# Linear attention and a routed FFN on one core: the bias added between scatter and return, and z of two batches computed ahead

## The chip, the core and the metric

The kernel runs on one core of a Trainium2 chip. The metric is the device time of one execution in microseconds. The engines are named as the profile names them: PE (TensorE, with PEld for its weight loads), DVE (VectorE), ACT (ScalarE), POOL (GpSimd) and SP (SyncE, which here only issues DMAs).

## What is computed

x is 4096 tokens of 128 numbers. Everything is float32.

```python
xn = layernorm(x)
# attention: 16 heads of 8 dims, 32 features a head; B = 16, T = 256
q, k, v = split(xn @ w_qkv)
q_prime = exp(z_q - max(z_q)), k_prime = exp(z_k - max(z_k))   # z = einsum('bhtd,hdf->bhtf', ., proj)
kv = einsum('bhtf,bhtd->bhfd', k_prime, v);  k_sum = sum(k_prime, axis=t)
att = (q_prime @ kv) / (q_prime @ k_sum + 1e-6);  A = att @ w_out + b_out
# FFN: 8 experts, 256 wide, Sinkhorn routing (3 iterations), top 2 of 8
gates = sinkhorn((xn @ router_w.T + router_b) / temp);  two best, weights sum to 1
F = xn + sum over the two of weight * ((relu(xn @ wg[e]) * (xn @ wp[e])) @ wo[e])
return x + A + F
```

## The kernel before

The 4096 tokens are 32 tiles of 128 (NT); a batch is two tiles, and there are 16 (NB). `acc` holds x of all tiles in SBUF and collects the result. Each engine runs its own list of instructions in program order and waits on semaphores; nothing is scheduled by a tool, so the order written in the code is the order that runs.

*Head (0 to 24 us).* x is loaded and normalised, xn is transposed and split in a high and a low part (three products make one product of nearly float32 precision), and the weights of the features are folded: `w_feat_high`, `w_feat_low`.

*Routing (24 to 60 us).* The Sinkhorn iterations and the top-2 choice are one chain of small instructions that goes round PE, DVE and ACT (`route_link`, links 0 to 17). It is interleaved with attention's steps for b = -1 and b = 0. At its end DVE places every token: `slot_i` gives each of the 2 x 4096 rows a slot in `slots_x` in HBM, sorted by expert, in 39 tiles of 256 slots (SLOT_TILES, ST).

*Attention (60 to 169 us).* `step(b, ...)` on each engine works on batch b and, ahead of it, on batch f = b + 1. In the names of the trace: `z(n, f)` is one of four groups of three 128x512 matmuls on PE (L618 to L620; n = 0, 1 for k, n = 2, 3 for q) into PSUM bank Z_BANK + n; DVE takes its negated maximum (`z_max`, L1058) and adds it (`z_shift`, L1065) into `z_sb`; ACT's exponential (`features`, L871) gives `feat`. For batch b, `kv(b)` is 16 matmuls of 36 columns (L642), `qT` transposes feat 2 and 3 (L656), ACT copies them out (`copy_qT`, L882), `numden(b)` is 16 matmuls of 36 columns (L666), DVE divides (`att`, L1080 to L1090) in the next step, PE transposes att (L673), ACT copies (L888), PE multiplies with w_out (`project`, L682) and DVE adds the product to `acc` (L1101, counted in `acc_added`). `kv(b)` waits for att of b - 1, since both use bank 6. 14 batches run so (EARLY); batches 14 and 15 run behind the experts.

Beside this, POOL scatters the rows: 64 indirect DMAs of 128 rows (L532), each followed by `add_xn`, half a tile of acc += xn (L491). Each waits on z_shifted, so that they keep pace with attention.

*Experts (169 to 272 us).* SP loads the weights of each tile's expert (`load_weights` into one of six `w_tile`, 384 KB) and its rows (`load_rows`, `x_tile`). PE transposes the rows and makes the up and gate products (L783 to L785) and the down product (L795); ACT splits (L948, L952), applies relu (L962) and scales the result into `y_tile` (L969, counted in `y_scaled`); DVE splits (L1262, L1281 `w_low`) and multiplies (L1270). POOL returns the rows: `send_rows(k)`, two indirect DMAs of 128 rows (L541) into `rows_y` in token order. Among them POOL adds the bias: 64 half tiles (`add_bias`, L496), one or two behind nearly every DMA, and a memset of one column of `gap` (L546) behind each tile. PE, ACT and DVE don't wait for a tile's return until 16 tiles later (YR).

*End (272 to 325 us).* PE runs attention's batches 14 and 15. SP waits for all returns (`y_sent`), reads both planes of rows back, POOL and DVE add them to acc (L327), and SP and ACT store it.

`keep_warm` (L574) is matmuls on constants whose result nobody reads.

## Time and profile before

| | us |
|---|---|
| median of 3 runs | 329.74 (328.19 to 330.65) |
| the profiled execution | 327.3 |
| its span in the trace | 325.5 |

| engine | busy us | share of the span | instructions |
|---|---|---|---|
| PE | 274.7 | 84% | 2044 |
| PEld | 257.5 | 79% | 2044 |
| DVE | 222.9 | 68% | 523 |
| ACT | 160.3 | 49% | 365 |
| POOL | 237.6 | 73% | 388 |

Of the chain of work that ended last, the page gives PE 49%, POOL 23%, DVE 12%, DMA 6%, ACT 2%. Times of a row are microseconds from the start of the span. An instruction's busy time on PE overlaps that of its neighbours, so the pace of PE is read from start to start. "PEclk" is the clock granted to PE as a share of 2.4 GHz.

### The profile page before, as it was taken

The numbers are of one execution on the slowest core, as the hardware profiler recorded it, in microseconds if no ns is written. First come the engines' busy times: TensorE is split into PE (matmuls) and PEld (weight loads), VectorE is DVE, ScalarE is ACT, GpSimd is POOL, SyncE is SP. The second block draws the span as 40 slices with busy tenths as digits, with TensorE's granted clock in tenths as the row PEclk, the third lists the DMA queues.
The fourth block names the chain that finished last, engine by engine and source line by source line (L and its number), as shares of the span: only waits on it lengthen the run. The fifth ranks groups of instructions, "written<-read, shape, count | busy, mean of one in ns | idle before, by whom it ended". The sixth has DMA issues, their size and how long they took to land.

```text
span 325.5 us, 6627 instructions
## 1 busy us (share of the span) xinstructions
PE 274.7 (84%) x2044; PEld 257.5 (79%) x2044; DVE 222.9 (68%) x523; ACT 160.3 (49%) x365; POOL 237.6 (73%) x388
## 2 busy tenths in 40 slices
PE   5996878799999999999699999999999999850020
PEld 4896777689999999999599999999999999850010
DVE  4948889668888778888855777777777774500173
ACT  2774562134555555455346677777777775210000
POOL 5899520757888888888611688888888888888381
PEclk9998996589999999999979999999999999885555
DMA  7974000551111111111142598898888841111694
GB/s 236 339 272 164 4 0 0 167 191 45 47 50 52 45 49 46 47 50 51 36 110 61 166 244 245 244 256 251 245 246 248 251 134 48 42 49 40 226 383 174
DMA packets 32462, 45.22 MB, mean 139 GB/s; under 512 B 5328, under 2 KB 21200, under 8 KB 32432
## 3 DMA queue, kind: packets, MB, share of 16 engines
q1 hardware_dynamic: 26592, 33.83, 34.1%
q0 software_dynamic: 4544, 9.84, 9.0%
q10 hardware_dynamic: 1296, 1.20, 1.1%
q8 instruction: 13, 0.21, 0.3%
q14 instruction: 17, 0.14, 0.1%
HBM read 27.17 MB, written 17.68 MB: 138 GB/s over the span
## 4 chain that ended last, share of the span: by engine, by line
PE 49%; POOL 23%; DVE 12%; DMA 6%; issue 5%; ACT 2%; SPq 1%; ACTq 0%; POOLq 0%; DVEq 0%
POOL rows_y L541 17%; PE bank L642 7%; PE bank L666 6%; POOL acc L496 5%; PE bank L618 4%; PE bank L619 4%; PE bank L620 4%; PE bank L656 4%; PE bank L795 3%; DMA xn<-rows_y 2%; PE bank L591 2%; PE bank L783 2%; PE bank L574 2%; PE bank L784 2%; PE bank L785 2%
## 5 line engine op out<-in xcount | busy, mean ns | idle before, releaser
L541 POOL DMA_INDIRECT rows_y<-xn,row_i x78 | 80.5, 1032 | 28.2 <-ACT xn L969 15.1
L532 POOL DMA_INDIRECT slots_x<-xn,slot_i x64 | 63.9, 999 | 29.4 <-DVE slot_i L1195 10.1
L871 ACT ACTIVATE feat<-z_sb 128x512 f32<-128x512 f32 x64 | 39.9, 631 | 65.7 <-DVE z_sb L1065 65.7
L1058 DVE TENSOR_REDUCE neg_max<-bank 128x16 f32<-128x512 f32 x64 | 42.7, 684 | 19.8 <-PE bank L620 19.8
L783 PE MATMUL bank<-xT_high,w_high 128*128 128x256 f32 x156 | 47.3, 303 | 0.5 <-issue 0.5
L785 PE MATMUL bank<-xT_high,w_low 128*128 128x256 f32 x156 | 44.0, 282 | 0.0
L784 PE MATMUL bank<-xT_low,w_high 128*128 128x256 f32 x156 | 44.0, 282 | 0.0
L1065 DVE TENSOR_TENSOR z_sb<-bank,neg_max 128x512 f32<-128x512 f32 x64 | 42.6, 684 | 0.5
L795 PE MATMUL bank<-w_tile,hidden 128*128 128x128 f32 x312 | 41.0, 275 | 0.0
L642 PEld LDWEIGHTS bank<-v_aug,feat 128*128 128x128 f32 x256 | 31.5, 200 | 8.8 <-issue 7.4
L795 PEld LDWEIGHTS bank<-w_tile,hidden 128*128 128x128 f32 x312 | 38.2, 192 | 0.1
L969 ACT ACTIVATE xn<-bank,x_tile 128x128 f32<-128x128 f32 x78 | 24.5, 365 | 25.8 <-PE bank L795 25.8
L642 PE MATMUL bank<-v_aug,feat 128*128 128x36 f32 x256 | 31.9, 283 | 5.7 <-DVE att L1090 5.7
L1281 DVE TENSOR_TENSOR w_low<-w_tile,w_high 128x512 fp32r<-128x512 f32 x39 | 28.5, 734 | 4.5 <-ACT w_high L952 1.2
L666 PE MATMUL bank<-kv_sb,qT_sb 128*128 128x36 f32 x256 | 31.6, 282 | 0.0
L666 PEld LDWEIGHTS bank<-kv_sb,qT_sb 128*128 128x128 f32 x256 | 31.5, 201 | 0.0
L1262 DVE TENSOR_TENSOR xT_low<-bank,xT_high 128x256 fp32r<-128x256 f32 x39 | 16.5, 424 | 21.8 <-ACT xT_high L948 21.8
L618 PE MATMUL bank<-w_feat_high,xnT_high 128*128 128x512 f32 x64 | 31.2, 487 | 0.0
L783 PEld LDWEIGHTS bank<-xT_high,w_high 128*128 128x128 f32 x156 | 29.6, 190 | 0.7 <-issue 0.7
L784 PEld LDWEIGHTS bank<-xT_low,w_high 128*128 128x128 f32 x156 | 29.8, 191 | 0.0
L785 PEld LDWEIGHTS bank<-xT_high,w_low 128*128 128x128 f32 x156 | 29.6, 190 | 0.0
L1270 DVE TENSOR_TENSOR hidden<-bank,gate_act 128x512 f32<-128x512 f32 x39 | 26.5, 680 | 3.2 <-PE bank L785 3.2
(145 smaller groups left out, 562.5 us busy)
## 6 DMA issues: line engine op xcount, KB each, us to landing
w_tile<-w_expert_dram SPq DMA_DIRECT2D x39, 384.0 KB
slots_x<-w_tile SPq DMA_DIRECT2D x39, 144.0 KB, 2.2
x_tile<-slots_x SPq DMA_DIRECT2D x39, 130.0 KB
acc<-x_dram SPq DMA_DIRECT2D x8, 256.0 KB, 5.3
xn<-rows_y SPq DMA_DIRECT2D x8, 256.0 KB, 5.8
w_tile<-rows_y SPq DMA_DIRECT2D x8, 256.0 KB, 6.5
rows_y<-xn,row_i POOLq DMA_INDIRECT x78, 3.7
slots_x<-xn,slot_i POOLq DMA_INDIRECT x64, 2.3
```

Source lines behind the costliest of these rows:

```text
L532: pool.indirect_dma_start(slots_x, bass.IndirectOffsetOnAxis(slot_i[k][:, i:i + 1], 0), xn[:, j, :], None).then_inc(scattered[n % FLIGHT], 16)
L541: pool.indirect_dma_start(rows_y, bass.IndirectOffsetOnAxis(row_i[:, k, t:t + 1], 0), y_tile(k, t), None)\
L618: pe.matmul(to, xT(xnT_high, f, half), w_feat_high[:, qk, :], start=True, stop=False)
L642: mm = pe.matmul(bank[KV_BANK][:, c * AUG:(c + 1) * AUG], feat[par][h][:, c * P:(c + 1) * P], v_aug[:, 2 * b + h, c * AUG:(c + 1) * AUG], ...
L666: mm = pe.matmul(bank[KV_BANK][:, at:at + AUG], qT_sb[h][:, c * P:(c + 1) * P], kv_sb[par][:, c, :], start=True, stop=True)
L783: pe.matmul(to, w_high[n][:, cols], xT_high[n][:, :], start=True, stop=False)
L784: pe.matmul(to, w_high[n][:, cols], xT_low[n][:, :], start=False, stop=False)
L785: mm = pe.matmul(to, w_low[n][:, cols], xT_high[n][:, :], start=False, stop=True)
L795: mm = pe.matmul(y_bank(r, t), hidden[r % UP][:, c, t * P:(t + 1) * P], w_tile[:, r, at:at + D], start=(c == 0), stop=(c == FC - 1))
L871: act.activation(feat[par][n][:, :], z_sb[n][:, :], ACT.Exp).then_inc(feat_ready, 1)
L1058: dve.tensor_reduce(neg_max[n][:, :], args(n), AX_X, ALU.max, negate=True).then_inc(z_negmax, 1)
L1065: dve.tensor_tensor(z_sb[n][:, :].rearrange("p (h f) -> p h f", f=F), args(n), wide(neg_max[n], F), ALU.add).then_inc(z_shifted, 1)
```

## The change

It has two parts.

The bias. `add_bias` becomes a group of four tiles (128x512), eight of them, which POOL runs behind the last `add_xn` and ahead of the first `send_rows`; the groups wait for acc_added 2, 4, ... 12, 13, 13. Between the return DMAs no bias add is left, and behind each of the 78 DMAs stands a memset of one column.

z of batches 4 and 9 (AHEAD). `z_ahead(i)`, i = 0 to 7, makes the eight groups of three matmuls in idle banks (QT_BANK, V_BANK) during routing: 0 to 2 ahead of the row transposes of the three iterations, 3 and 4 behind the transposes of batch 0, 5 to 7 behind numden(0). ACT copies each to SBUF (`store_ahead`): batch 4 into w_tile, batch 9 into hidden and gate_act. In the attention stage `z(n, 4)` and `z(n, 9)` are left out on PE, and DVE reads the stored ones. SP's first weight load now waits for z_shifted 20 (batch 4's z used up), since it overwrites the store.

```diff
+    AHEAD = (4, 9)
-        gap = sb("gap", [P, SLOT_TILES])
+        gap = sb("gap", [P, 2 * SLOT_TILES])
+        z_store = [flat_w[:, FEAT * (n + 1):FEAT * (n + 2)] for n in range(4)]
+        z_store += [t[:, :, :].rearrange("p c s -> p (c s)") for t in hidden] + [gate_act[1][:, :]]
...
+            sp.wait_ge(z_shifted, 4 * (AHEAD[0] + 1))
             for k in range(LOOP):
                 load_weights(*ahead(k, 0, 0))
...
-            def add_bias(n):
-
-                j, cols = half_tile((n + 4 * (EARLY - 1)) % (2 * NT))
-                pool.tensor_tensor(acc[:, j, cols], acc[:, j, cols], b_out_sb[:, cols], ALU.add).then_inc(bias_added, 1)
+            def add_bias(g):
+
+                tiles = acc[:, g * GROUP:(g + 1) * GROUP, :]
+                pool.tensor_tensor(tiles, tiles, over_tiles(b_out_sb, GROUP), ALU.add).then_inc(bias_added, 1)
...
-                    n = 2 * k + t
-                    for piece in range(n * NT // SLOT_TILES, (n + 1) * NT // SLOT_TILES):
-                        add_bias(piece)
-                pool.memset(gap[:, k:k + 1], 0.0)
+                    pool.memset(gap[:, 2 * k + t:2 * k + t + 1], 0.0)
 
             pool.wait_ge(base_added, 2 * NT)
+            for g in range(NG):
+                pool.wait_ge(acc_added, min(GROUP // 2 * (g + 1), EARLY - 1))
+                add_bias(g)
             pool.wait_ge(acc_added, EARLY - 1)
...
             def z(n, f):
 
+                if f in AHEAD:
+                    return
...
+            def z_ahead(i):
+
+                n, f = i % 4, AHEAD[i // 4]
+                pe.wait_ge(xnT_split, f // 2 + 1)
...
+                z_products(n, f, z_ahead_bank(i)[:, :]).then_inc(z_ahead_ready, 1)
...
                     values(2 * (n // 5))
+                    z_ahead(n // 5)
                     pe.wait_ge(row_normed, n // 5 + 1)
...
                 if back:
                     qT(0, b, par, route)
+                if back and route:
+                    z_ahead(3)
...
                 if back:
                     qT(1, b, par, route)
+                if back and route:
+                    z_ahead(4)
...
                 if back:
                     numden(b, par)
+                if back and route:
+                    for i in range(5, 8):
+                        z_ahead(i)
...
+            def store_ahead(i):
+
+                act.wait_ge(z_ahead_ready, i + 1)
+                act.copy(z_store[i], z_ahead_bank(i)[:, :]).then_inc(z_ahead_stored, 1)
...
-            def args(n):
-                return bank[Z_BANK + n][:, :].rearrange("p (h f) -> p h f", f=F)
+            def args(n, f):
+                z = z_store[4 * AHEAD.index(f) + n] if f in AHEAD else bank[Z_BANK + n][:, :]
+                return z.rearrange("p (h f) -> p h f", f=F)
```

Of PE's list, the second half of step 3 (batch 3, ahead of it f = 4), before: the last of att's transposes, then the transposes of feat 2 and 3 with z(2) and z(3) between them, the projection, and numden of batch 3.

```order
L673 MATMUL bank0<-ident,att 128x128 x2
L656 MATMUL bank5<-ident,feat1_2 128x128 x4
L618 MATMUL bank3<-w_feat_high,xnT_high 128x512
L619 MATMUL bank3<-w_feat_low,xnT_high 128x512
L620 MATMUL bank3<-w_feat_high,xnT_low 128x512
L656 MATMUL bank7<-ident,feat1_3 128x128 x4
L618 MATMUL bank4<-w_feat_high,xnT_high 128x512
L619 MATMUL bank4<-w_feat_low,xnT_high 128x512
L620 MATMUL bank4<-w_feat_high,xnT_low 128x512
L682 MATMUL bank5<-w_out_sb,attT 128x128 x2
L666 MATMUL bank6<-kv_sb1,qT_sb0 128x36 x4
```

Both z groups are gone from here, and so are z(0) and z(1), which stood between numden of batch 2 and kv of batch 3; the same holds for step 8. In the changed kernel PE goes from numden(2) straight to kv(3).

Of PE's list in step 0, behind kv(0), now: the transposes of feat 3 (L695), then z_ahead(4), the two products of the routing counts (L735, L736), numden(0) (L705), and the first of z_ahead(5) to (7), ahead of z(0) and z(1) of batch 2.

```order
L695 MATMUL bank<-ident,feat_3 128x128 x4
L653 MATMUL bank<-w_feat_high,xnT_high 128x512
L654 MATMUL bank<-w_feat_low,xnT_high 128x512
L655 MATMUL bank<-w_feat_high,xnT_low 128x512
L735 MATMUL bank<-mask,earlier_r 128x256
L736 MATMUL bank<-mask,ones_r 128x256
L705 MATMUL bank<-kv_sb,qT_sb 128x36 x8
L653 MATMUL bank<-w_feat_high,xnT_high 128x512
L654 MATMUL bank<-w_feat_low,xnT_high 128x512
L655 MATMUL bank<-w_feat_high,xnT_low 128x512
```

Before, the counts followed the transposes at once, and behind numden(0) stood only the six matmuls of z(0) and z(1); now there are fifteen.

Of POOL's list in the middle of the expert stage, before: return DMAs (L541), bias adds of half a tile (L496), and the memset behind a tile (L546).

```order
L541 DMA rows_y<-xn,row_i 18176x128
L496 TENSOR_TENSOR acc<-acc,b_out_sb 128x64
L546 MEMSET gap 128x1
L541 DMA rows_y<-xn,row_i 18176x128 x2
L496 TENSOR_TENSOR acc<-acc,b_out_sb 128x64
```

And the same list now, with its start:

```order
L506 TENSOR_TENSOR acc<-acc,xn 128x64
L511 TENSOR_TENSOR acc<-acc,b_out_sb 128x512 [waits acc_added,base_added]
L511 TENSOR_TENSOR acc<-acc,b_out_sb 128x512 [waits acc_added] x7
L556 DMA rows_y<-xn,row_i 18176x128 [waits y_scaled,rows_numbered,acc_added]
L558 MEMSET gap 128x1
L556 DMA rows_y<-xn,row_i 18176x128
L558 MEMSET gap 128x1
L556 DMA rows_y<-xn,row_i 18176x128 [waits y_scaled,rows_numbered]
```

The 64 small adds have become eight large ones ahead of the first return, and the memsets are 78 instead of 39.

## Rows read from the trace of the kernel before

**Rows 1.** Busy time by stages: stretch, its length, engines, PEclk, DMA share, GB/s

```profile
60.20:169.10 108.90, 106.17 (x748) 97.13 (x748) 85.60 (x169) 51.05 (x94) 83.82 (x130) 0.95 0.22 70
169.10:272.00 102.90, 102.28 (x881) 101.80 (x880) 72.53 (x156) 73.29 (x191) 80.99 (x135) 1.00 0.73 210
272.00:302.20 30.20, 16.40 (x118) 15.24 (x117) 7.40 (x15) 5.89 (x12) 25.46 (x47) 0.80 0.14 44
```

**Rows 2.** POOL's timeline (start, duration, line, tiles, idle before): tiles 0, 1, 38

```profile
177.61 0.98 POOL L541 DMA_INDIRECT rows_y<-xn,row_i  x1 [12.74 <-ACT xn L969]
...
182.41 0.98 POOL L541 DMA_INDIRECT rows_y<-xn,row_i  x1 [2.10 <-ACT xn L969]
...
298.44 0.99 POOL L541 DMA_INDIRECT rows_y<-xn,row_i  x1 [0.16 <-issue]
```

**Rows 3.** ACT's timeline: y of two tiles in a row, and of tile 38

```profile
250.16 0.63 ACT L969 ACTIVATE xn<-bank,x_tile 128x128 f32<-128x128 f32 x2 [0.64 <-PE bank L795]
...
252.71 0.63 ACT L969 ACTIVATE xn<-bank,x_tile 128x128 f32<-128x128 f32 x2 [0.64 <-PE bank L795]
...
272.24 0.63 ACT L969 ACTIVATE xn<-bank,x_tile 128x128 f32<-128x128 f32 x2 [0.42 <-PE bank L795]
```

**Rows 4.** POOL's timeline: two return DMAs with only the memset between

```profile
276.32 0.99 POOL L541 DMA_INDIRECT rows_y<-xn,row_i  x1 [0.17 <-issue]
277.32 0.11 POOL L546 MEMSET gap<- 128x1 f32 x1
277.62 0.96 POOL L541 DMA_INDIRECT rows_y<-xn,row_i  x1 [0.19 <-issue]
```

**Rows 5.** Timeline of all engines: a return DMA behind DVE's w_low

```profile
213.40 0.69 DVE L1281 TENSOR_TENSOR w_low<-w_tile,w_high 128x512 fp32r<-128x512 f32 x1
213.57 1.39 POOL L541 DMA_INDIRECT rows_y<-xn,row_i  x1 [0.16 <-issue]
```

**Rows 6.** DVE's timeline: the first add of returned rows

```profile
307.66 0.89 DVE L327 TENSOR_TENSOR acc<-xn,acc 128x512 f32<-128x512 f32 x1 [19.86 <-DMA xn<-rows_y]
```

**Rows 7.** Groups of POOL by form: count | busy, mean ns | idle before

```profile
L327 POOL TENSOR_TENSOR acc<-xn,acc 128x512 f32<-128x512 f32 x4 | 5.7, 1414 | 5.5 <-DMA xn<-rows_y 5.4
```

**Rows 8.** PE's timeline in a steady step: numden, z(0), kv, next numden

```profile
107.91 1.87 PE L666 MATMUL bank<-kv_sb,qT_sb 128*128 128x36 f32 x16
109.61 0.48 PE L618 MATMUL bank<-w_feat_high,xnT_high 128*128 128x512 f32 x1
...
111.09 1.87 PE L642 MATMUL bank<-v_aug,feat 128*128 128x36 f32 x16
...
115.75 0.42 PE L666 MATMUL bank<-kv_sb,qT_sb 128*128 128x36 f32 x3
```

**Rows 9.** Who waited for whom: total us, times, longest

```profile
PE bank L701 <- DVE row_log L1143: 4.8, 3, 2.5
```

**Rows 10.** PE in two stretches: length, PE busy, PEclk, DMA share, GB/s

```profile
51.00:68.00 17.00, 14.56 (x56) 0.50 0.41 140
283.00:286.50 3.50, 3.50 (x18) 0.51 0.12 37
```

**Rows 11.** PE's timeline: kv(1) and numden(1)

```profile
60.21 3.60 PE L642 MATMUL bank<-v_aug,feat 128*128 128x36 f32 x16 [1.80 <-DVE att L1090]
...
68.66 1.87 PE L666 MATMUL bank<-kv_sb,qT_sb 128*128 128x36 f32 x16
```

**Rows 12.** Timelines of DVE and ACT in the steady step: att, the second qT copy

```profile
110.43 0.42 DVE L1090 TENSOR_TENSOR att<-bank,inv_den 128x256 f32<-128x256 f32 x1
...
114.81 0.59 ACT L882 COPY qT_sb<-bank 128x512 f32<-128x512 f32 x1
```

**Rows 13.** PE's timeline: numden(14), kv(15), numden(15)

```profile
278.10 1.87 PE L666 MATMUL bank<-kv_sb,qT_sb 128*128 128x36 f32 x16
...
281.19 1.95 PE L642 MATMUL bank<-v_aug,feat 128*128 128x36 f32 x16 [1.22 <-DVE att L1090]
...
287.85 1.87 PE L666 MATMUL bank<-kv_sb,qT_sb 128*128 128x36 f32 x16
```

More of the change, by code:

```diff
@@ L251, in by_token_tile, with z_ahead_bank, in_psum @@
             return t.rearrange("p (j d) -> p j d", d=P)
+        flat_w = w_tile[:, :, :].rearrange("p r n -> p (r n)")
+        z_store = [flat_w[:, FEAT * (n + 1):FEAT * (n + 2)] for n in range(4)]
+        z_store += [t[:, :, :].rearrange("p c s -> p (c s)") for t in hidden] + [gate_act[1][:, :]]
+        def z_ahead_bank(i):
+            return bank[QT_BANK if i < 3 or i % 2 == 1 and i > 4 else V_BANK]
+        def in_psum(f):
+            return f - sum(1 for a in AHEAD if a < f)
         def v_bank(g):
@@ L934, in step @@
                     copy_qT(0, b, route)
+                if back and route:
+                    store_ahead(3)
                 if tail:
@@ L938, in step @@
                     copy_qT(1, b, route)
+                if back and route:
+                    for i in range(4, 8):
+                        store_ahead(i)
                 if front and not route:
@@ L1097, in add_projection @@
                 dve.wait_ge(base_added, 4 * b + 4)
[L1098 to L1099 removed]
+                if b == EARLY - 1:
+                    dve.wait_ge(bias_added, NG)
                 tiles = acc[:, bass.ds(2 * b, 2), :]
```

40 lines of the change are left out of this document (29 added, 11 removed).

## The prediction

> **What bounds the kernel now.** I read the table by stages first. The attention stage (60.2 to 169.1 us) has PE busy 106.17 of 108.90 us, the expert stage PE 102.28 of 102.90 us, and behind it stand 30.2 us with PE busy 16.40 us and POOL 25.46 us [rows 1], then, up to 325.5, 23.3 us of reading back, adding and storing. So two things decide: when the experts can start (PE in the attention stage), and when POOL has sent the last of the 39 tiles' rows back. POOL's timeline shows that it is POOL, not PE, that ends the expert stage: tile 0 is sent at 177.61 after 12.74 us of idling, tile 1 at 182.41, tile 38 at 298.44, while ACT had tile 38 ready at about 272.87 [rows 2, 3]. Between tiles 1 and 38 lie 37 tiles in 116.03 us, 3.136 us each; PE makes one in 2.55 us (252.71 less 250.16). POOL falls some 25 us behind.
>
> **Term A, the returns.** A tile is two indirect DMAs. 64 of the 78 DMAs have a bias add behind them; where only the memset stands there, the way from DMA to DMA, 276.32 to 277.62, is 1.30 us [rows 4]. The change leaves only that form: 2.60 us a tile. On top come collisions: the DMA at 213.57 started inside DVE's w_low (213.40, 0.69 us, both inputs in SBUF) and took 1.39 instead of 0.99 us [rows 5]. At 2.60 us against DVE's 2.55 the two drift by 0.05 us a tile, so that one of the two DMAs of a tile runs into w_low about every 6 to 12 tiles and pays 0.4 to 0.6 us: 0.06 us a tile. I take 2.66: 37 x (3.136 - 2.66) = **-17.6 us**. Bounds: no collisions, 2.60, -19.8 us; one hit of 0.40 in every tile, 3.00, -5 us. PE doesn't cap it (2.55 is less), nor does what comes after: DVE's first add of returned rows, at 307.66, comes after 19.86 us of idling [rows 6]. The Trainium skill (SBUF — State Buffer, "SBUF: two separate sides") has the pair of ports that DVE and GpSimd share as a lock held for the whole instruction against a DVE instruction with two SBUF inputs; the row of 1.39 us agrees, and by that rule too the sum stays near 2.66 a tile.
>
> The eight bias adds now stand between the last scatter's add and tile 0. POOL's nearest form, 128x512 with two inputs, takes 1.41 us [rows 7]: 11.3 us, six of which may start at once, two when acc_added reaches 13. They fall into the 12.74 us that POOL idles [rows 2]. Cost nothing; if they run 2 us over, tile 1 still comes 4.8 us after tile 0 and takes it up.
>
> **Term B, the routing.** Eight z products are added (24 matmuls, a group of three is 0.70 us, from half of the 1.48 us between 109.61 and 111.09, [rows 8]) and eight ACT copies of 0.57 us. Three groups stand ahead of the row transposes, where PE waits 4.8 us in three waits [rows 9]: hidden, and the copies fit into ACT's gaps. The other five stand between the transposes of batch 0 and the z of batch 2, while DVE is placing the slots. There PE now runs at 1.2 GHz: the granted clock is 0.50 from 51 to 68 us [rows 10], so that kv(1) at 60.21 needs until numden at 68.66 to arrive, 8.45 us where the same way takes 4.66 (111.09 to 115.75) [rows 8, 11]. If the added matmuls hold the clock, up to 3.8 us come back; if it falls anyway, nine more matmuls at 0.43 us end about 62, 1.8 us after kv(1) wants to start. I take **-1.5 us**. The weight loads now wait for z_shifted 20, some 30 us later; they are wanted at 157.
>
> **Term C, batches 4 and 9 without z on PE.** The intent is 12 matmuls less, 2.9 us, in a PE-bound step of 7.85 us (107.91 to 115.75) [rows 8]. But look at who waits in the step. z(0) and z(1) run from 109.61 to 111.09 [rows 8]; kv behind them also waits for att, which DVE ends at 110.85 [rows 12]. Taking the six away brings kv 0.15 us forward. The same with z(2), z(3): numden waits for ACT's second qT copy, which stands in ACT's order behind two exponentials and two copies; it ended at 115.40 [rows 12], against numden at 115.75, and could go 0.25 us earlier. So the step sheds 0.5 us, not 2.9. DVE's own work doesn't get less: it reads z from SBUF instead of PSUM, same shapes.
>
> What it does to the clock is worse. Without z a step is numden, a gap, kv, a few transposes, a gap, numden. The trace has one such step, batch 15: numden(14) at 278.10, 1.22 us idle, kv at 281.19, numden(15) at 287.85: **9.75 us, longer than a step with z (7.85)**, though six filling matmuls stand in for the twelve of z [rows 13]. The granted clock is 0.51 from 283.0 to 286.5, right behind numden, gap and kv [rows 10]. The other low stretch, 51 to 68, was not ended by the z of batch 2, between a numden and a kv at half clock, and ended in the dense run of transposes and z of batch 2 ahead of numden(1). In the middle of the attention stage a fallen clock hits a PE-bound stretch: numden +1.7, the next z(0), z(1) +1.4, kv +1.7, the rest up to z(3) about +2 until the clock is back. That is 3 to 8 us a time; less the 0.5 us shed, I take +5 a batch, **+10 us** for both. Bounds per batch: -0.5 (no fall) and +8.
>
> The Trainium skill (TensorE: Matmul & The Clock Gate, "HAM oscillation") ties the fall to PE standing idle between bursts of matmuls. In a step without z PE would still be busy most of the time, and by that rule alone the clock holds; batch 15's rows say otherwise. What the rule gives is the first rival.
>
> **Sum.** 327.3 (the profiled execution; span 325.5) - 17.6 - 1.5 + 10 = 318.2 us. That execution lies 2.4 us under the median of the three timed ones (329.74), so for a median I say **320 us**.
>
> **Rivals.**
> *The clock holds in both batches*: C is -1, and B nearer -2.5: 327.3 - 17.6 - 2.5 - 1 = 306.2, 308.5 for a median. For it: a steady step keeps 1.00 with numden and kv in it. Against: batch 15.
> *The clock falls and stays down over whole steps* (slower than before): every us at half clock costs 0.5 us of a PE-bound stage, so 38 us of low clock eat the 19 us won. In the trace the longest low stretch is 17 us; two of 30 us, from numden and kv of a following batch keeping it down, would give 327.3 - 19.1 + 30 = 338.
> *The returns don't get faster*: as POOL sends faster the DMA engines, busy 0.73 in the expert stage [rows 1], deliver x_tile rows late and PE paces at 3 us, or collisions hit every tile: A is -5 or less: 327.3 - 5 - 1.5 + 10 = 330.8, 332 for a median.
>
> **Chances.** My forecast (returns faster, clock falls at 4 and 9) 0.60, clock holds 0.23, stays down 0.08, returns no faster 0.09. About 1% is what a measurement of this kernel can tell from no change. The forecast's own range is 312 (both falls short) to 327 (both long, A at -15). The overall range must reach the first rival: 307 to 328. Faster by over 1% (below 326.4): 0.56 + 0.23 = 0.79; within 1%: 0.04 + 0.08 = 0.12; slower: 0.08 + 0.01 = 0.09.
>
> **What would show it.** A: return DMAs 1.30 us apart, POOL done about 7 us behind ACT's last y rather than 26. B: the clock of 51 to 68 and the distance from kv(1) to numden(1). C: the distance from numden(2) to numden(3) and to numden(4), and the granted clock there: 7.4 and 7.85 at full clock mean the first rival, 9 and 12 or more mean my step. The end of the attention stage (PE's filling matmuls, 169.1) should come about 8 us later; if it comes earlier than 168, term C is wrong. If the DMAs stay 1.5 us apart, term A is.

## The result, and the profile after

The changed kernel takes **348.31 us** (median of 4 executions, 340.10 to 353.88) where the kernel before, run beside it, takes 328.97 (327.89 to 330.65): ratio **1.041, 95% interval 1.026 to 1.056**. Ratios, here and below, leave out executions more than 1.5% above the fastest of their kernel (here 353.88, the profiled one, and 351.71; the other two, 340.10 and 344.92, give 1.041), while medians have all of them. It is slower; 320 us and "faster" were predicted. The experiments showed more than that sign. They ran on five chips (which chip the two kernels of this section ran on is not known). On one of them the same changed kernel is 4% *faster* than the kernel before, and on another its bias part alone is 6% faster. What differs between the chips is the subject of most of what follows.

The profiled execution of after has 353.88 us (span 352.1, mean granted clock 0.890), that of before had 327.3 (0.909). The first view to read is, in both, the line that scales an expert tile's result on ACT: its group says when the first and the last of the 78 halves started. Before:

```profile
L969 ACT ACTIVATE xn<-bank,x_tile x78: 358/365/370, 176.2 to 272.5; 128x128 f32<-128x128 f32 x78
```

The same line of after, and who it waited for (total us, times):

```profile
L1029 ACT ACTIVATE xn<-bank,x_tile x78: 358/368/407, 191.6 to 318.5; 128x128 f32<-128x128 f32 x78
its engine sat idle before it (us, times) until:
  PE bank L844: 18.1, 14
  remote: 17.2, 10
```

The extra 26.6 us of this execution fall into three pieces. The first scaled tile comes 15.4 us later (191.6 against 176.2), which is the attention stage. From the first to the last scaling it takes 126.9 us in place of 96.3, 30.6 more. And from there to the end it takes 33.6 us in place of 53.0, 19.4 less, since POOL is no longer far behind. 15.4 + 30.6 - 19.4 = 26.6.

The attention stage on PE, where [rows 11] and [rows 8] answer (start, duration, group of matmuls, idle before; L677 is kv, L705 numden, L589 the filling matmuls at the stage's end):

```profile
59.03 2.94 PE L677 MATMUL bank<-v_aug,feat 128*128 128x36 f32 x16 [2.51 <-DVE att L1154]
...
66.99 1.87 PE L705 MATMUL bank<-kv_sb,qT_sb 128*128 128x36 f32 x16
...
74.83 1.87 PE L705 MATMUL bank<-kv_sb,qT_sb 128*128 128x36 f32 x16
...
77.93 1.95 PE L677 MATMUL bank<-v_aug,feat 128*128 128x36 f32 x16 [1.22 <-DVE att L1154]
...
82.77 3.47 PE L705 MATMUL bank<-kv_sb,qT_sb 128*128 128x36 f32 x16
...
97.46 1.87 PE L705 MATMUL bank<-kv_sb,qT_sb 128*128 128x36 f32 x16
```

And PE in four stretches of after (length, busy us of PE, PEld, DVE, ACT, POOL, granted clock as a share of 2.4 GHz, DMA share, GB/s), where [rows 1] and [rows 10] answer:

```profile
59.80:66.60 6.80, 6.80 (x28) 6.11 (x28) 3.17 (x6) 3.20 (x6) 4.33 (x8) 0.50 0.14 47
80.20:97.30 17.10, 16.95 (x69) 15.28 (x68) 8.82 (x18) 6.39 (x13) 10.04 (x16) 0.50 0.51 174
124.60:145.10 20.50, 20.41 (x85) 18.74 (x85) 10.64 (x20) 7.16 (x13) 12.15 (x18) 0.50 0.10 34
184.70:318.50 133.80, 110.35 (x880) 105.70 (x880) 70.44 (x156) 73.86 (x192) 82.84 (x149) 0.97 0.56 166
```

Behind batch 2 and behind batch 7 the clock falls to 1.2 GHz and stays there for 17.1 and 20.5 us, with PE busy throughout. In the last row PE is busy 110.35 of 133.80 us: in the expert stage, where it was never idle before, it now waits for 23 us, with the clock at 0.97 and with the DMA engines less busy than before (0.56; 0.77 from 176.0 to 272.5 before).

POOL does what the change is for. Its timeline, where [rows 2] and [rows 4] answer, and two of the waits:

```profile
178.71 9.90 POOL L511 TENSOR_TENSOR acc<-acc,b_out_sb 128x512 f32<-128x512 f32 x8
193.02 0.98 POOL L556 DMA_INDIRECT rows_y<-xn,row_i  x1 [4.41 <-ACT xn L1029]
194.00 0.12 POOL L558 MEMSET gap<- 128x1 f32 x1
194.31 0.96 POOL L556 DMA_INDIRECT rows_y<-xn,row_i  x1 [0.19 <-issue]
```

```profile
POOL rows_y L556 <- ACT xn L1029: 38.8, 28, 4.4
```

The eight adds take 9.90 us inside POOL's idle time, the return DMAs stand 1.29 us apart, and POOL now waits for scaled tiles (38.8 us in 28 waits) where it had been 25 us behind them.

### The profile page after: what moved, and what is told of

It reads as the page before. It is cut to its first block, busy times and chain, and to the rows that moved or that the text cites. A ratio compares the mean times of both kernels' runs of the same rounds, so it can differ in the third digit from the quotient of the medians.

```text
span 352.1 us, 6625 instructions
## 1 busy us (share of the span) xinstructions
PE 298.9 (85%) x2044; PEld 275.5 (78%) x2044; DVE 220.8 (63%) x523; ACT 165.6 (47%) x373; POOL 227.8 (65%) x371
## 4 chain that ended last, share of the span: by engine, by line
PE 56%; DVE 15%; ACT 10%; issue 9%; another core or an unknown queue 6%; DMA 3%; ACTq 0%; DVEq 0%
PE bank L677 9%; PE bank L705 6%; PE bank L844 5%; PE bank L695 4%; PE bank L653 4%; PE bank L655 4%; PE bank L654 3%; PE bank L832 3%; PE bank L834 3%; PE bank L833 3%; PE bank L589 2%; ACT xn L1029 2%; ACT w_high L1012 2%; PE bank L723 2%
## 5 line engine op out<-in xcount | busy, mean ns | idle before, releaser
L556 POOL DMA_INDIRECT rows_y<-xn,row_i x78 | 75.7, 971 | 51.9 <-ACT xn L1029 38.8
L1122 DVE TENSOR_REDUCE neg_max<-bank 128x16 f32<-128x512 f32 x56 | 37.6, 685 | 27.3 <-PE bank L655 27.2
L832 PEld LDWEIGHTS bank<-xT_high,w_high 128*128 128x128 f32 x156 | 30.3, 194 | 26.2 <-DVE xT_low L1326 19.5
L677 PEld LDWEIGHTS bank<-v_aug,feat 128*128 128x128 f32 x256 | 38.0, 233 | 11.6 <-issue 9.8
L677 PE MATMUL bank<-v_aug,feat 128*128 128x36 f32 x256 | 38.2, 314 | 9.0 <-DVE att L1154 9.0
L1129 DVE TENSOR_TENSOR z_sb<-bank,neg_max 128x512 f32<-128x512 f32 x56 | 37.2, 682 | 0.4
L705 PE MATMUL bank<-kv_sb,qT_sb 128*128 128x36 f32 x256 | 33.3, 290 | 1.9 <-ACT qT_sb L936 1.9
L705 PEld LDWEIGHTS bank<-kv_sb,qT_sb 128*128 128x128 f32 x256 | 33.2, 210 | 2.1 <-ACT qT_sb L936 2.1
L653 PE MATMUL bank<-w_feat_high,xnT_high 128*128 128x512 f32 x64 | 32.6, 510 | 0.1
L1022 ACT ACTIVATE gate_act<-bank 128x512 f32<-128x512 f32 x39 | 23.7, 607 | 17.9 <-PE bank L834 11.2
L936 ACT COPY qT_sb<-bank 128x512 f32<-128x512 f32 x32 | 18.6, 582 | 27.0 <-PE bank L695 24.0
L834 PEld LDWEIGHTS bank<-xT_high,w_low 128*128 128x128 f32 x156 | 30.6, 196 | 0.0
```

What stands on the lines that cost most here:

```text
L556: pool.indirect_dma_start(rows_y, bass.IndirectOffsetOnAxis(row_i[:, k, t:t + 1], 0), y_tile(k, t), None)\
L653: pe.matmul(to, xT(xnT_high, f, half), w_feat_high[:, qk, :], start=True, stop=False)
L677: mm = pe.matmul(bank[KV_BANK][:, c * AUG:(c + 1) * AUG], feat[par][h][:, c * P:(c + 1) * P], v_aug[:, 2 * b + h, c * AUG:(c + 1) * AUG], ...
L705: mm = pe.matmul(bank[KV_BANK][:, at:at + AUG], qT_sb[h][:, c * P:(c + 1) * P], kv_sb[par][:, c, :], start=True, stop=True)
L832: pe.matmul(to, w_high[n][:, cols], xT_high[n][:, :], start=True, stop=False)
L834: mm = pe.matmul(to, w_low[n][:, cols], xT_high[n][:, :], start=False, stop=True)
```

## The experiments

The trace also holds a record of each semaphore increment. I read `y_ready`, which the last matmul of a tile's `down` raises, and call a tile's signal late when the increment comes more than 0.45 us behind that matmul's end. (In before it comes 0.29 us behind the matmul's start, which is its end, in all 39 tiles; where the expectations give 0.29 us as behind the end, they are loose.) ScalarE's scaling and SyncE's next weight load both wait for it. After has 19 late signals of 39, by 38 us in sum. Where records of `y_ready` are missing (1 in after, up to 5 in before_third, ahead_only, ahead_only_again and bias_dummy_adds), an increment is matched to the nearest matmul, so a count or a sum there can be off by a few. "Remote" as a releaser stands in such rows where the profile could join the increment to no matmul, since it came too long behind its end: bias_only has it 13 times in front of the scaling, and all its records of `y_ready`.

### One part at a time

bias_only: the kernel before with the bias part alone.

```diff
+            for g in range(NG):
+                pool.wait_ge(acc_added, min(GROUP // 2 * (g + 1), EARLY - 1))
+                add_bias(g)
...
-                    for piece in range(n * NT // SLOT_TILES, (n + 1) * NT // SLOT_TILES):
-                        add_bias(piece)
-                pool.memset(gap[:, k:k + 1], 0.0)
+                    pool.memset(gap[:, 2 * k + t:2 * k + t + 1], 0.0)
```

> The kernel before with the change's bias part alone: the eight bias adds between scatter and return, a one-column memset behind each of the 78 return DMAs, and no z ahead of its turn. In the trace of the changed kernel the expert stage on TensorE takes 133 us in place of 103, and TensorE's signals there (y_ready by line 844) reach ScalarE 2 to 3 us after the matmuls end in 19 of 39 tiles, where the kernel before has 0.29 us in all 39. Theory R (the returns that now follow each scaled tile in step disturb this stage): this kernel shows the same late signals, an expert stage of 120 to 133 us, and a time of 325 to 345 us although the returns start earlier. Theory Z (z ahead of its turn, or the clock that falls behind it, is the cause of all of it): an expert stage of 103 us, returns 2.66 us a tile, and about 312 us, the 17.6 us of the prediction's first term off the 329.

Measured: **340.71 us** against 331.12 (ratio 1.027, 1.016 to 1.037), 18 late signals, scalings from 178.5 to 307.5. Theory R: the steps of the attention stage take 7.84 us as before, and the part that I had counted on for -17.6 us costs 10.

ahead_only: the changed kernel with the bias adds back among the returns.

```diff
-            for g in range(NG):
-                pool.wait_ge(acc_added, min(GROUP // 2 * (g + 1), EARLY - 1))
-                add_bias(g)
...
-                    pool.memset(gap[:, 2 * k + t:2 * k + t + 1], 0.0)
+                    n = 2 * k + t
+                    for piece in range(n * NT // SLOT_TILES, (n + 1) * NT // SLOT_TILES):
+                        add_bias(piece)
+                pool.memset(gap[:, k:k + 1], 0.0)
```

> The changed kernel with its bias part undone: the bias adds stand among the returns as before, one memset for a pair of return DMAs, but z of batches 4 and 9 is still computed during routing. Theory R: no late signals in the expert stage, which takes 103 us again; what is left is the slower attention stage (+15.4 us in the trace of the changed kernel) less 1.7 us of routing, so about 340 to 345 us. Theory Z: the expert stage stays at 120 to 133 us and the time is 350 us or more.

Measured: 336.50 us (ratio 1.013, 1.000 to 1.026), and 22 late signals, scalings from 181.1 to 302.7. So neither theory as I had put it: without the bias part the signals are late as well, and the time is still under 340.

bias_only_one_gap: as bias_only, with one memset for a pair of return DMAs.

```diff
-                    pool.memset(gap[:, 2 * k + t:2 * k + t + 1], 0.0)
+                pool.memset(gap[:, k:k + 1], 0.0)
```

> The bias part alone as in the run bias_only, but with one memset behind each pair of return DMAs, as in the kernel before, in place of one behind each. Theory R in its form that the return DMA right behind a scaled tile is the trouble: late signals and a long expert stage as in bias_only, within 3 us. In the form that the second memset is the trouble: an expert stage of 103 us and a time 5 us or more under bias_only's. Theory Z: 103 us as in bias_only, and the same time within 1 us.

Measured: 339.15 us (ratio 1.025), 16 late, scalings 128.1 us from first to last (bias_only 129.0). The second memset is not the trouble. Theory R, in its form with the return right behind a scaled tile, stands; its other form falls.

ahead_refilled: the changed kernel, with PE computing the products of batches 4 and 9 again in their old places, for nobody.

```diff
                 if f in AHEAD:
+                    pe.wait_ge(z_shifted, 4 * (f - 1) + n + 1)
+                    z_products(n, f, bank[Z_BANK + n][:, :])
                     return
```

> The changed kernel, but TensorE computes the products of batches 4 and 9 a second time in their old places (12 matmuls each, into the banks of z, read by nobody), so that the attention steps ask as much of TensorE as before. If the granted clock falls because TensorE has less to do in steps 3 and 8, the spacing from numden(3) to numden(4) and from numden(8) to numden(9) goes back from 14.7 to about 8 us, the clock stays at 1.00 there, and the attention stage loses the 15.4 us it had gained. If something else slows those steps (VectorE reading z from SBUF, the copies on ScalarE), they stay at 14.7 us. For the expert stage theory R expects the late signals as in the changed kernel (133 us), so 333 to 338 us in all; theory Z expects 103 us, so 308 to 313 us.

Measured: 347.16 us, no better than the changed kernel. The distances between the last matmuls of successive numdens say more (us; in brackets how much of it the clock was low; ahead_only on the chip of ahead_refilled):

| kernel | (2)-(3) | (3)-(4) | (4)-(5) | (7)-(8) | (8)-(9) | (9)-(10) |
|---|---|---|---|---|---|---|
| before | 7.84 | 7.84 | 7.85 | 7.90 | 7.84 | 7.84 |
| after | 9.40 (5.6) | 13.22 (11.5) | 7.85 | 11.05 (9.0) | 13.22 (11.5) | 7.85 |
| ahead_only | 10.12 | 9.27 | 7.84 | 7.56 | 9.44 | 7.85 |
| ahead_refilled | 7.85 | 8.98 | 13.34 (10.2) | 7.88 | 7.84 | 9.35 |

Thirteen more traces of kernels without z ahead read like before, but for two steps of 8.4 us. With the products refilled, both slow stretches are gone, behind batch 2 and behind batch 7, and the clock is full in them. In after it was low there for 17.1 and 20.5 us; in ahead_only, the nearer neighbour, for 10.3 and 3.4 us. So it is the clock that makes these steps slow, and with the matmuls in place it does not fall there. But a new fall comes in (4)-(5), and it has another origin. PE's timeline of ahead_refilled (L707 is numden, L679 kv) and one of its stretches:

```profile
81.21 1.87 PE L707 MATMUL bank<-kv_sb,qT_sb 128*128 128x36 f32 x16
...
90.09 1.98 PE L707 MATMUL bank<-kv_sb,qT_sb 128*128 128x36 f32 x16 [0.88 <-issue]
95.17 3.60 PE L679 MATMUL bank<-v_aug,feat 128*128 128x36 f32 x16 [0.94 <-DVE att L1156]
103.53 1.87 PE L707 MATMUL bank<-kv_sb,qT_sb 128*128 128x36 f32 x16
```

```profile
92.60:102.80 10.20, 9.26 (x36) 7.86 (x35) 5.02 (x10) 2.72 (x6) 4.47 (x8) 0.50 0.10 36
```

PE idles in front of numden(4), then in front of kv(5), and the clock falls between the two. Two signals of TensorE are late ahead of it: the transposes end at 88.06 us and ScalarE's copy starts at 89.45, the projection ends at 89.21 and VectorE's add starts at 91.00. The expected 333 to 338 us were missed by 9 us and more: what this kernel should have won it loses again here and in the expert stage, which takes 129.0 us from first to last scaling; why that is 2 us longer than in after is open.

### Is it the kernel?

All four variants had late signals, the one without the bias part too. Only the kernel before had none, and it had been traced on another occasion. So it ran again, at first beside a kernel with a single edit.

> The kernel before, unchanged, taken once more beside the others. In the traces of the changed kernel and of all four single-part variants the expert stage shows late signals of TensorE (y_ready 2 to 3 us after the matmuls end, in 16 to 22 of 39 tiles), and the time is 334 to 345 us; the trace of the kernel before shows none in 39. If the late signals are of the kernel (theory R or any other on the change), this run shows none again, 0.29 us in all 39 tiles, and an expert stage of 103 us. If they are of the occasion on which a trace is taken (theory O), this run shows them as well, with a span of 335 us or more where its trace was 325.5.

```diff
                     for piece in range(n * NT // SLOT_TILES, (n + 1) * NT // SLOT_TILES):
                         add_bias(piece)
-                pool.memset(gap[:, k:k + 1], 0.0)
+                    pool.memset(gap[:, 2 * k + t:2 * k + t + 1], 0.0)
```

> The kernel before with one edit of the change alone: a one-column memset behind each return DMA in place of one behind each pair; the bias adds stay among the returns. By the rows of before (the memset 0.1 us, with 0.2 us around it) a tile's returns take 3.14 + 0.3 = 3.4 us in place of 3.14 if nothing else changes, which makes the last return some 10 us later and the kernel 10 us slower (340). If a memset behind the DMA saves the following instruction what the change's returns save (1.30 us from DMA to DMA), it is 3.14 us again and 330 us. If theory R holds in the form that a memset between two DMAs disturbs TensorE's signals, the late signals appear here too.

Measured, on a second chip: before_again 325.44 us and no late signal; before_two_gaps 326.52 us, no late signal, ratio 1.002 (0.999 to 1.005): the extra memset costs nothing that can be measured. That spoke for the kernel as the cause. But these were another chip than that of the four variants, so the next four ran together.

> The kernel before, unchanged, beside the three below on one chip. So far late signals of TensorE in the expert stage (2 to 3 us after the matmuls) stand in every trace of a changed kernel or of one of its parts, and in no trace of the kernel before, but the two kinds of trace were taken on different occasions and chips. Theory K (it comes of the kernel): none here, whatever the runs below show. Theory O (it comes of the chip or occasion): this trace and the three below agree, all with late signals or all without. With late signals its expert stage on TensorE would be about 125 to 130 us in place of 103, yet its time about 330 us, since its returns take 122.6 us for themselves and hide up to 20 us of that.

> The changed kernel once more, on the chip of the kernel before. Theory K: late signals, an expert stage near 130 us, 340 to 350 us. Theory O, if the occasion has none: an expert stage of 103 to 105 us; what is left is the clock in the attention stage, and the time is 318 to 328 us, near the prediction; if the occasion has them: 340 to 350 us with late signals in the kernel before as well.

> The bias part alone once more, on the chip of the kernel before. Theory K: late signals in 16 or more of 39 tiles and 338 to 344 us. Theory O, if the occasion has none: an expert stage of 103 us, returns 2.66 us a tile, and 309 to 314 us, the prediction's first term off the kernel before; if it has them: about 340 us.

> The part on z alone once more, on the chip of the kernel before. Theory K: late signals and 334 to 340 us. Theory O, if the occasion has none: returns 3.14 us a tile as before, so the kernel before plus what the attention stage gains by the clock less 1.7 us of routing: 328 to 340 us.

Measured, on a third chip: after_again 344.62 us (ratio 1.047, 1.038 to 1.057), bias_only_again 341.31 (1.040), ahead_only_again 343.05 (1.020), with 19, 18 and 15 late signals; and **the kernel before, unchanged, has 19 late signals too**, at 331.45 us. Its scaling line and two of its waits:

```profile
L969 ACT ACTIVATE xn<-bank,x_tile x78: 357/367/404, 175.8 to 297.1; 128x128 f32<-128x128 f32 x78
```

```profile
POOL rows_y L541 <- ACT xn L969: 20.1, 6, 12.7
ACT xn L969 <- remote: 12.6, 7, 2.4
```

From 175.8 to 297.1 are 121.3 us in place of 96.3, and yet the time is within 1% of the other traces of this kernel. The returns hide it: 116.03 us for tiles 1 to 38 [rows 2] are nearly as long. Theory O: it is not of the kernel, and the time of the kernel before does not betray it. Each chip was used on one occasion only, but for the second, which showed no late signal on either of two; so whether it is the chip, or something else on it at that hour, is not separated, and "chip" below means both.

### What the late signals come with

Three kernels ran together on a fourth chip. small_weight_loads is the bias part with weight loads of 8 columns from tile 6 on (a tile's 384 KB are 768 columns; the 1536 in the expectation are wrong).

```diff
-                sp.dma_start(w_tile[:, r, :], w_expert[e, :, :].rearrange("a p n -> (a p) n"))\
+                few = slice(0, 8) if late(k, LOOP) else slice(0, 3 * FF)
+                sp.dma_start(w_tile[:, r, few], w_expert[e, :, few].rearrange("a p n -> (a p) n"))\
```

> The bias part alone, but the weight loads of tiles 6 to 38 bring 8 columns (4 KB) in place of 1536 (768 KB by the tile, 384 KB of them by the profile's row); the tiles then work with weights of earlier ones. Read only where the trace shows the records lost in the attention stage, as every trace with late signals does. Theory M (TensorE's signals are late where loads fill the DMA engines): no late signals in the expert stage, scaled tiles 2.55 us apart, the stage 96 us from the first to the last of them in place of 128.5, and returns 2.66 us a tile: 308 to 315 us. Theory P (they come of the returns): late signals as in bias_only and 120 us or more.

Measured: 336.32 us (ratio 1.027), 18 late. The stretch of its scalings:

```profile
176.00:302.00 126.00, 99.72 (x823) 95.64 (x822) 65.61 (x145) 71.28 (x187) 78.91 (x143) 1.00 0.27 74
```

The DMA engines are busy 0.27 of the time, and the stage is as long as ever. Theory M falls: it is not the traffic of the weight loads.

returns_after: the bias part, with the return DMAs behind the last scaled tile.

```diff
-                pool.wait_ge(y_scaled, k + 1)
+                pool.wait_ge(y_scaled, SLOT_TILES)
...
-                if late(k, YR):
-                    act.wait_ge(y_sent[k % YR], 2 * 16 * (k // YR))
```

> The bias part alone, but POOL sends no tile back before the last is scaled, and ScalarE does not wait for its buffers (the returned values are then mostly those of later tiles): the expert stage runs with its loads and no return DMA. Theory P: no late signals, 96 us from the first to the last scaled tile. Theory M: late signals remain in 15 or more of 39 tiles, and the stage is 115 us or more. Either way the 78 return DMAs behind it add about 39 x 2.6 = 101 us, so 400 to 430 us in all; only the stage is read.

Measured: no late signal in the stage, 95.7 us from first to last scaling, on the same chip (405.58 us in all, as the returns stand behind):

```profile
L967 ACT ACTIVATE xn<-bank,x_tile x78: 358/364/368, 173.5 to 269.2; 128x128 f32<-128x128 f32 x78
```

With [rows 3] this is the pace of 2.55 us a tile again. Theory P: **the late signals come with POOL's return DMAs.** This edit takes away at once POOL's issuing, the rows' transfer to HBM and ScalarE's wait for it, so which of them it is stays open.

bias_dummy_adds: the bias part, with adds of the old shape into a spare tile among the returns.

```diff
-                    pool.memset(gap[:, 2 * k + t:2 * k + t + 1], 0.0)
+                    for piece in range(n * NT // SLOT_TILES, (n + 1) * NT // SLOT_TILES):
+                        if piece:
+                            pool.wait_ge(spare_added, piece)
+                        pool.tensor_tensor(spare[:, :], b_out_sb[:, 0:D // 2], b_out_sb[:, D // 2:D], ALU.add)\
+                            .then_inc(spare_added, 1)
+                pool.memset(gap[:, 2 * k:2 * k + 1], 0.0)
```

> The bias part alone, but with 64 adds of the old shape (128x64, into a spare tile) among the return DMAs where the bias adds stood, and one memset per pair: the returns get their old pace back, 3.1 us a tile, and nothing else changes. If the bias part makes the expert stage longer because the return DMAs now stand closer together and right behind each scaled tile, this kernel's stage goes back from 128.5 to 121 us and the time from 341 to 330. If it is the eight large adds ahead of the returns or where the bias is added, it stays at 128 us and 340.

Measured: 328.93 us (ratio 1.003, 0.999 to 1.006), the time of before; 14 late signals by 23 us in sum, where small_weight_loads on the same chip has 18 by 38; scalings 104.6 us from first to last, less than the 121 expected. The eight large adds stand where they stand in the change, so they are not the cost; what costs is how close the return DMAs stand to each other and to the scaling. The bias part itself, with full loads, did not run on this chip, so its price there is taken from small_weight_loads (126.0 us). Why the returns at the old pace leave 104.6 us here and 121.3 in the kernel before on the third chip is open.

### Without late signals

> The bias part alone, on another occasion. Where the trace loses semaphore records in the attention stage (as in all traces with late signals): late signals in 16 or more of 39 tiles, a stage of 128 us from first to last scaled tile and 338 to 344 us. Where it loses none: the prediction's first term alone, no late signals, 96 us from first to last scaled tile, 309 to 314 us.

Measured, on the second chip again: **306.32 us** against 325.86, ratio **0.943 (0.936 to 0.950)**, no late signal. Its scaling line, and the last tile's two returns on POOL:

```profile
L969 ACT ACTIVATE xn<-bank,x_tile x78: 359/365/370, 175.3 to 271.9; 128x128 f32<-128x128 f32 x78
```

```profile
276.83 0.96 POOL L541 DMA_INDIRECT rows_y<-xn,row_i  x1 [0.19 <-issue]
277.79 0.11 POOL L543 MEMSET gap<- 128x1 f32 x1
278.10 0.96 POOL L541 DMA_INDIRECT rows_y<-xn,row_i  x1 [0.19 <-issue]
```

POOL is done about 7 us behind the last scaling, as the prediction said. The same kernel with and without late signals, side by side: PE's `down` (L795), POOL's returns, ACT's scaling and SyncE's next weight load, first bias_only, then bias_only_third.

```profile
187.29 1.06 PE L795 MATMUL bank<-w_tile,hidden 128*128 128x128 f32 x8
...
188.49 0.96 POOL L541 DMA_INDIRECT rows_y<-xn,row_i  x1 [0.19 <-issue]
...
189.83 1.06 PE L795 MATMUL bank<-w_tile,hidden 128*128 128x128 f32 x8
190.54 0.62 ACT L969 ACTIVATE xn<-bank,x_tile 128x128 f32<-128x128 f32 x2 [2.79 <-remote]
190.67 0.35 SPq L379 DMA_DIRECT2D w_tile<-w_expert_dram  x1
```

```profile
186.68 1.06 PE L795 MATMUL bank<-w_tile,hidden 128*128 128x128 f32 x8
...
187.77 0.63 ACT L969 ACTIVATE xn<-bank,x_tile 128x128 f32<-128x128 f32 x2 [0.63 <-PE bank L795]
187.88 0.96 POOL L541 DMA_INDIRECT rows_y<-xn,row_i  x1 [0.19 <-issue]
187.90 0.36 SPq L379 DMA_DIRECT2D w_tile<-w_expert_dram  x1
```

Without: scaling 1.09 us behind the start of `down`. With: 3.25 us, while PE has gone on to the next tile's transposes, its `up` and the next `down` (189.83). The work is done in time, and only word of it comes late, to two engines at once, 1.09 us after the second return DMA ends on POOL (189.45). The Trainium skill (Perfetto Trace Analysis, "Summary: the profiler window per engine type") says that TensorE's rows have an estimated end and leave out the way of its semaphore; these rows agree: what the group of `down` does not show is nothing in one trace and 2.2 us in the other (188.35, its end, to 190.54).

returns_lag: the bias part, POOL four tiles behind.

```diff
-                pool.wait_ge(y_scaled, k + 1)
+                pool.wait_ge(y_scaled, min(k + 1 + 4, SLOT_TILES))
```

> The bias part alone, but POOL sends tile k back only when tile k + 4 is scaled (the last ones when the last is scaled). The return DMAs keep their pace, and stand no longer right behind the scaling of their own tile, but still behind that of another, so a late signal still delays the next return and the return's end the next signal. If the lockstep of returns and scaled tiles costs the 7 us between 121 and 128.5 us whatever tile is sent, the stage stays at 128 us, and the end comes later by four tiles' returns, 4 x 2.6 = 10 us: about 350 us. If it mattered that a tile is sent while its successor's signals are due, the stage falls to 121 us or less and the time is near 340. Without late signals: about 320.

Measured, on the second chip: 315.67 us (ratio 0.970), no late signal: 9.4 us more than bias_only_third for the lag, the 10 us expected. It ran on no chip with late signals, and so does not answer the question that it asks.

one_return: in the stage only the first return DMA of each tile.

```diff
-            for k in range(SLOT_TILES):
-                send_rows(k)
+            for t in range(2):
+                for k in range(SLOT_TILES):
+                    send_rows(k, (t,))
...
-                    act.wait_ge(y_sent[k % YR], 2 * 16 * (k // YR))
+                    act.wait_ge(y_sent[k % YR], 16 * (k // YR))
```

> The bias part alone, but in the expert stage only the first of each tile's two return DMAs is issued; the 39 second ones follow behind the last scaled tile (their values are then mostly those of later tiles). If every return DMA holds TensorE's signals back, half the lateness is left: 9 or more late tiles and a stage of 105 to 115 us. If it takes a second DMA within 1.3 us of the first (the signals come back about 1 us behind the end of the second one in the trace of bias_only), no signal is late and the stage is 96 us. The second DMAs add some 39 x 1.3 = 51 us behind the stage.

Measured there as well: 348.35 us, no late signal. Where bias_only has none either, that tells nothing on late signals; the second DMAs behind the stage cost 42 us, less than the 51 worked out.

> The whole change on another occasion. Where the trace shows no late signals: the bias part's 306.3 us plus the attention stage's 15.4 us less 0 to 1.7 us of routing, so 320 to 323 us, 1 to 2% under the kernel before on the same chip (325.9), and slow steps at numden(3) to (4) and (8) to (9) by the clock. Where it does: 342 to 350 us, as twice before.

Measured, on a fifth chip without late signals: **312.48 us** against 325.65, ratio **0.960 (0.952 to 0.967)**, scalings 97.4 us from first to last. The expectation of 320 to 323 was 8 us too high, since in the profiled execution (310.73 us) the clock fell for 3.4 us only behind batches 2 and 7, not for 17 and 20:

```profile
80.50:83.90 3.40, 3.30 (x16) 2.90 (x16) 2.89 (x6) 2.69 (x6) 3.01 (x5) 0.50 0.12 43
124.90:128.30 3.40, 3.40 (x12) 2.82 (x12) 2.29 (x6) 0.03 (x1) 3.01 (x5) 0.50 0.12 43
```

> The bias part with returns four tiles behind the scaling. Without late signals 315.7 us again. With them: if the lockstep of a tile's return with its own scaling makes the stage longer than 121 us, the stage from first to last scaled tile is 121 us or less here and the time 340 or less; if the return DMAs hold the signals back wherever they stand, it is 128 us as in bias_only, and 350 us.

Measured on the fifth chip: 315.77 us (0.970), the number of the second chip again. The late signals that it was to meet did not come. The changed kernel is 3.3 us faster than this, the bias part alone, on the second chip, 6 us faster than the changed kernel.

All in one table (scalings: first to last of the 78 starts, from each trace):

| late signals | before's scalings, time | bias part | z part | whole change |
|---|---|---|---|---|
| none (2nd, 5th chip; first trace of before) | 96.3 to 96.6, 325.5 to 325.9 us beside them | 96.6 us, ratio 0.943 (2nd) | not run | 97.4 us, 0.960 (5th) |
| yes (1st, 3rd, 4th chip; trace of after) | 121.3 (3rd), 327.7 to 331.1 us | 128.1 to 129.0 us, 1.025 to 1.040 | 121.6 and 121.7 us, 1.013 and 1.020 | 126.9 and 131.4 us, 1.041 and 1.047 |

## Why the prediction was wrong, point by point

**What bounds the kernel.** "It is POOL, not PE, that ends the expert stage" was right for the trace that I had, and so was "PE makes one in 2.55 us". The failed step is the sentence in term A that took this as a property of the kernel: **"PE doesn't cap it (2.55 is less)"**. Where the signals come late, PE makes a tile in 121.3 / 38 = 3.2 us in the kernel before, as slow as the returns' 3.136. POOL's 25 us of lag were the room in which this could stand unseen: in before_third POOL ends 6.4 us behind the last scaling, in the first trace 28.4. Taking POOL's bound away laid it open, for with returns that need 2.60 us a tile the bias part takes 129.0 / 38 = 3.4. Whether the 3.2 of before_third are a pace of PE's own, or PE held in step by POOL, the runs don't separate.

**Term A** (-17.6, bounds -19.8 and -5). Mechanism and size were right where no signal is late: 325.86 to 306.32 is -19.5 us. The 2 us more are the collisions: none of the 78 return DMAs of bias_only_third takes over 1.2 us, where before has 11, and POOL keeps PE's 2.55 us a tile. With late signals it is +9.6 (1st chip) and +11.9 us (3rd), outside any bound that I gave. The eight adds cost nothing, as said: 9.90 us within POOL's idle time.

**Term B** (-1.5). kv(1) comes at 59.03 in place of 60.21 and numden(1) at 66.99 in place of 68.66: -1.7, the size forecast. But that is no more than the scatter: the three traces of the kernel before and before_two_gaps have numden(1) at 67.48 to 68.66, and kernels without z ahead at 66.03 to 69.69 in all. So the term is not shown. The clock still fell, at 59.8 in place of 51.

**Term C** (+10, +5 a batch; bounds -0.5 and +8 a batch). The mechanism is what the rows show: PE idles 1.22 us in front of kv(3), as in front of kv(15) [rows 13], and the clock falls. From numden(2) to (4) it takes 22.6 us in place of 15.7, from (7) to (9) some 24.3 in place of 15.7: +6.9 and +8.5, together 15.4, near the upper bounds. This is the profiled execution, the slowest of four. The 17.1 and 20.5 us stand also in after_again and ahead_only_again, whose mean clocks are 0.887 and 0.882. In ahead_only, with a clock of 0.920, the two ways are +3.7 and +1.3, in after_third (0.934) +0.5 and +1.2. The other timed executions of after have no trace, but one sum fits: 353.88 (clock 0.890) less 340.10 (0.937) is 13.8 us, and 15.4 less the 1.7 of after_third is 13.7. So I estimate that C costs about 2 us in the 340.10, and that what makes that execution slower than before is the late signals. What I mis-sized is how long a fallen clock stays: "the rest until the clock is back" was about 2 us, and it was back after 17 to 20 us, 10.3 or 3.4. Why is open. The late signals alone are not the reason, since on the fifth chip one execution without a trace took 324.15 us with a clock of 0.89, beside 310.73 to 313.21. The Trainium skill (TensorE: Matmul & The Clock Gate, "HAM oscillation") ties a fall to waits for DMAs that are longer than the bursts of matmuls between them. The 1.22 us in front of kv(3) stand behind a numden of 1.87 us and ahead of a kv of 1.95, so this case does not bear that out, and the 17 us at half clock with PE busy 16.95 of 17.10 us are not explained by it either.

**The rivals.** "The returns don't get faster" had the right place, "PE paces at 3 us", and a chance of 0.09; but I had it from x_tile rows landing late under more traffic, and small_weight_loads refutes the loads' traffic. It also left a gain of 5 us where there was a loss of 10, because it kept the 96.3 us as PE's floor. "The clock stays down over whole steps" (0.08) is what the profiled execution shows, two low stretches of 17.1 and 20.5 us, near the 38 us that the rival wanted for eating the gain; the faster executions don't bear it out. For "the longest low stretch is 17 us" I had overlooked the end of the trace of before, where the clock is at 1.2 GHz from 293.3 us to the end, 32 us, with PE nearly idle. "The clock holds" is near after_third: 308.5 for 312.5.

**The sum.** 318.2 for an execution of 327.3 is -9.1; without late signals -13.2 was measured (325.65 to 312.48): A 2 us better, B and C together +6.2 in place of +8.5, by difference between two chips. That the two are near is in part luck: the rows of after_third have +1.7 for C, not +10, and 1.6 us stand in no term, the way from numden(12) to numden(13), 14.0 us in all five traces with z left out and 12.4 in bias_only_third. With late signals, in the profiled execution: C +15.4, B -1.7, 1.7 more on the way to the first scaling, the scalings +30.6, the returns' lag given back -19.4.

**What would show it.** "DMAs 1.30 us apart" and "POOL done about 7 us behind" came true on every chip that the bias part or the whole change ran on (6.5 to 7.8 us), and saved no time where the signals are late. I had named signs for each step of the change, and none for the engine that I took to be idle in reserve: its own pace.

## What to carry to other kernels

Before taking a bound away, ask what stands right under it, and whether that was measured or only not visible: an engine that is 25 us ahead of the bound lost 25 us on another chip here, and the time did not show it. Read the trace of the unchanged kernel from more than one chip, and compare the pace of the engines that don't bind, not the times. And price a part on the chip by itself: here the bias part alone (306.3 us) beats both kernels where no signal is late and loses to the one before on the two other chips that it ran on, while z ahead of its turn gained on neither chip that it ran on alone, both with late signals.

## What the runs showed of the hardware

- TensorE's semaphore increments can come 1 to 3 us behind the end of the matmul in place of with it (4.4 us at most in the traces that have every record of `y_ready`, in small_weight_loads), while the next matmuls are running. In the expert stage this comes with POOL's indirect DMAs (none of 39 tiles without them), not with the traffic of the weight loads (18 of 39 at a DMA share of 0.27). Three chips showed it in every kernel that had the returns in the stage, two in none. On those three the trace also loses 16 to 44% of the engines' semaphore records in stretches with POOL's indirect DMAs, from 60 us on, and none of 413 in the stage of returns_after, without them; on the other two it loses 8% at most. Whether both have one cause, whether the recording itself delays the signals (every timed execution has a recorded span and clock), and what in the chip differs, is open: no run was without the recording.
- On such a chip return DMAs 1.3 us apart cost more than ones 1.5 us or more apart (38 against 23 us of lateness on the fourth chip). In bias_only 14 of the 18 late signals come 0.95 to 1.07 us behind the end of a tile's second DMA, and the next return waits for that signal; that this loop is what makes 129 us of 121 is argued from the pattern, not shown, as returns_lag met no late signals.
- One and the same program left TensorE's clock at 1.2 GHz for 17.1 and 20.5 us in an execution with a mean clock of 0.890, and for 3.4 and 3.4 us in one with 0.934, in the same two places, with PE busy in all of them.
